# Three buffers for the slots' gathered rows and one for their outputs, in place of two and two

## What is computed

```python
def _L0_ffn_ref(x, gate_w, w1, b1, w2, b2, shared_w1, shared_b1, shared_w2, shared_b2):
    xf = x.reshape(-1, D)                      # 2048 rows of 512
    logits = xf @ gate_w
    top_logits, top_idx = jax.lax.top_k(logits, K)       # K = 2 of 8 experts
    top_gates = jax.nn.softmax(top_logits, axis=-1)
    ...
    h = gelu(jnp.einsum('nd,edh->neh', xf, w1) + b1)     # hidden size 256
    out_e = jnp.einsum('neh,ehd->ned', h, w2) + b2
    routed = jnp.einsum('ne,ned->nd', gates, out_e)
    shared = gelu(xf @ shared_w1 + shared_b1) @ shared_w2 + shared_b2
    return (routed + shared).reshape(B, S, D)
```

## Time and profile before

| what | us |
|---|---|
| median of three runs | 1681.28 |
| lowest and highest of them | 1679.48, 1681.79 |
| the profiled execution, device time | 1685.41 |
| its span, first to last instruction | 1683.7 |
| stage of the slots, from the first gather to the last y_out | 215.9 to 398.4 |

### The profile page before, as it was taken

The page is one execution under the profiler, slowest core; times in us unless marked ns, Lnnn a source line. Parts: engine busy times, 40 slices in busy tenths (PEclk is TensorE's granted clock), DMA queues, the critical chain, the costliest instruction groups (busy, mean ns, idle before and its releaser), DMA issues.

```text
span 1683.7 us, 27163 instructions
## 1 busy us (share of the span) xinstructions
PE 1626.0 (97%) x9136; PEld 1334.5 (79%) x9136; DVE 1084.2 (64%) x2115; ACT 1105.8 (66%) x2983; POOL 488.2 (29%) x515
## 2 busy tenths in 40 slices
PE   7989979999999999999999999999999999999998
PEld 6878756666778888888888888788888788887887
DVE  6258845443996668777787776666666666788322
ACT  4364245553468988888888888787787787885100
POOL 1001123222524243343342432433433334331000
PEclk9999979999999999999999999999999999999999
DMA  7031638885773242373333353121152131110011
GB/s 270 26 107 51 256 133 299 302 302 177 262 238 119 82 161 84 132 294 125 132 139 130 132 224 121 56 89 56 49 201 102 39 113 56 38 45 1 25 38 38
DMA packets 75156, 220.72 MB, mean 131 GB/s; under 512 B 6368, under 2 KB 14560, under 8 KB 68640
## 3 DMA queue, kind: packets, MB, share of 16 engines
q1 hardware_dynamic: 69360, 200.61, 32.7%
q0 software_dynamic: 5680, 18.62, 3.6%
HBM read 158.65 MB, written 60.56 MB: 130 GB/s over the span
## 4 chain that ended last, share of the span: by engine, by line
PE 72%; DMA 6%; DVE 5%; ACT 4%; issue 1%; POOL 1%; ACTq 0%; DVEq 0%; POOLq 0%; SPq 0%
PE bank L2485 10%; PE bank L2486 10%; PE bank L2548 7%; PE bank L97 6%; PE bank L99 6%; PE bank L98 6%; PE bank L2566 6%; PE bank L2579 6%; DMA s_rows<-x_rows,t_tok 5%; PE bank L2537 5%; PE bank L2558 3%; PE bank L1396 2%; PE bank L1416 2%; DVE x_res L1754 1%; PE bank L1376 1%
## 5 line engine op out<-in xcount | busy, mean ns | idle before, releaser
L2817 DVE TENSOR_TENSOR t_hn<-bank,t_rs 128x256 f32<-128x256 f32 (+1 forms) x256 | 130.8, 553 | 138.7 <-POOL t_rs L2450 73.2
L2485 PE MATMUL bank<-t_slot,t_x_q 128*128 128x512 f32 x512 | 205.8, 402 | 0.0
L2447 POOL TENSOR_SCALAR t_ve<-t_ss 128x4 f32<-128x4 f32 (+1 forms) x128 | 26.1, 204 | 615.5 <-DVE t_ss L2813 608.0
L2486 PE MATMUL bank<-t_slot,t_x_q 128*128 128x512 f32 x512 | 200.3, 391 | 0.0
L2706 ACT ACTIVATE t_sc<-bank,t_mx 128x128 f32<-128x128 f32 x512 | 184.4, 456 | 3.2 <-DVE t_mx L2837 3.2
L2450 POOL TENSOR_TENSOR t_rs<-t_ve,t_mhalf 128x4 f32<-128x4 f32 (+1 forms) x128 | 171.2, 1337 | 10.7
L2706 ACT ACTIVATION_READ_ACCUMULATOR t_sc<-bank,t_mx 128x1 f32 x512 | 151.8, 296 | 0.0
L2744 ACT ACTIVATE t_y<-bank,smooth 128x128 bf16<-128x128 f32 x512 | 139.7, 402 | 1.9 <-PE bank L2566 1.9
L2548 PEld LDWEIGHTS bank<-t_hT 128*128 128x128 f32 x1024 | 120.0, 191 | 17.0 <-ACT t_hT L2733 16.5
L2548 PE MATMUL bank<-t_hT 128*128 128x128 f32 x1024 | 131.0, 281 | 2.3 <-ACT t_hT L2733 2.3
L2486 PE MATMUL bank<-t_slot,t_x_kv 128*128 128x256 f32 x512 | 125.6, 283 | 0.0
(11 more groups left out here) (344 smaller groups left out, 4165.5 us busy)
## 6 DMA issues: line engine op xcount, KB each, us to landing
t_slot<-w_ready SPq DMA_DIRECT2D x16, 2048.0 KB, 9.3
t_xh<-xq_scratch SPq DMA_DIRECT2D x64, 512.0 KB, 3.6
t_cr<-in_ctxT_dram SPq DMA_DIRECT2D x64, 256.0 KB, 2.7
y_rows<-s_y SPq DMA_DIRECT2D x39, 256.0 KB
e_w<-in_w_units_dram SPq DMA_DIRECT2D x8, 1024.0 KB, 12.2
w_rows<-in_w_qkv_dram SPq DMA_DIRECT2D x8, 1024.0 KB, 6.2
w_ready<-w_hi SPq DMA_DIRECT2D x8, 1024.0 KB, 5.0
w_ready<-w_lo SPq DMA_DIRECT2D x8, 1024.0 KB
```

What stands on the lines that cost most here:

```text
L2485: nc.tensor.matmul(out, x_in[:, k, :], w[0][:, k, a:b], start=k == 0, stop=False)
L2486: last = nc.tensor.matmul(out, x_in[:, k, :], w[1][:, k, a:b], start=False, stop=k == KT - 1)
L2817: nc.vector.tensor_tensor(hn[:, lo:hi, :], b3[bk][:, 0:hi - lo, :], rs[:, lo:hi].unsqueeze(2).broadcast_to([P, hi - lo, P]), ALU.mult).the ...
```

## The change

The bytes are the same: three `rows` buffers (152, 154, 168) and one `y` buffer (170) take the place of two and two. The gather of slot s waits for turn(s-3) instead of turn(s-2). `y_out(s)` waits for the landing of the store of slot s-1 instead of s-2. One more semaphore counts the third gather buffer. No instruction changes its place on any engine; only buffers, semaphores and what is waited for differ.

```diff
-        self.rows = [mem.at(f"s_rows{i}", 152 + 2 * i, [P, D]) for i in range(2)]
+        self.rows = [mem.at(f"s_rows{i}", kb, [P, D]) for i, kb in enumerate((152, 154, 168))]
...
-        self.y = [mem.at(f"s_y{i}", 168 + 2 * i, [P, D]) for i in range(2)]
-        (rows_in0, rows_in1, self.turned, self.xT_in, self.up_ps, self.h_in, self.hturned, self.g_in, self.y_ps, self.y_in,
+        self.y = mem.at("s_y", 170, [P, D])
+        (rows_in0, rows_in1, rows_in2, self.turned, self.xT_in, self.up_ps, self.h_in, self.hturned, self.g_in, self.y_ps, self.y_in,
...
         for s in range(SLOTS_N):
-            if s >= 2:
-                pool.wait_ge(self.turned, s - 1)
+            if s >= 3:
+                pool.wait_ge(self.turned, s - 2)
             self.nc.gpsimd.indirect_dma_start(
-                self.rows[s % 2][:], None, self.env.dram["x_rows"],
-                bass.IndirectOffsetOnAxis(ap=self.route.tok[:, s:s + 1], axis=0)).then_inc(self.rows_in[s % 2], 16)
+                self.rows[s % 3][:], None, self.env.dram["x_rows"],
+                bass.IndirectOffsetOnAxis(ap=self.route.tok[:, s:s + 1], axis=0)).then_inc(self.rows_in[s % 3], 16)
 
     def turn(self, pe, s):
-        pe.wait_ge(self.rows_in[s % 2], 16 * (s // 2) + 16)
+        pe.wait_ge(self.rows_in[s % 3], 16 * (s // 3) + 16)
...
         def y_out(s):
             act.wait_ge(self.y_ps, s + 1)
-            if s >= 2:
-                act.wait_ge(self.y_st[s % 2], 16 * (s // 2))
-            nc.scalar.activation(self.y[s % 2][:], env.bank[6 + s % 2][:], ACT.Copy).then_inc(self.y_in, 1)
+            if s >= 1:
+                act.wait_ge(self.y_st[(s - 1) % 2], 16 * ((s - 1) // 2 + 1))
+            nc.scalar.activation(self.y[:], env.bank[6 + s % 2][:], ACT.Copy).then_inc(self.y_in, 1)
...
-            sp.dma_start(self.env.dram["y_rows"][s * P:(s + 1) * P, :], self.y[s % 2][:]).then_inc(self.y_st[s % 2], 16)
+            sp.dma_start(self.env.dram["y_rows"][s * P:(s + 1) * P, :], self.y[:]).then_inc(self.y_st[s % 2], 16)
```

More of the change, by code:

```diff
@@ L1351, in __init__ @@
         self.hT = [mem.at(f"s_hT{i}", 162 + i, [P, HT, P]) for i in range(2)]
-        self.y = [mem.at(f"s_y{i}", 168 + 2 * i, [P, D]) for i in range(2)]
-        (rows_in0, rows_in1, self.turned, self.xT_in, self.up_ps, self.h_in, self.hturned, self.g_in, self.y_ps, self.y_in,
+        self.y = mem.at("s_y", 170, [P, D])
+        (rows_in0, rows_in1, rows_in2, self.turned, self.xT_in, self.up_ps, self.h_in, self.hturned, self.g_in, self.y_ps, self.y_in,
          y_st0, y_st1) = (ctx.enter_context(nc.semaphore("s_" + n)) for n in (
-             "rows_in0", "rows_in1", "turned", "xT_in", "up_ps", "h_in", "hturned", "g_in", "y_ps", "y_in",
+             "rows_in0", "rows_in1", "rows_in2", "turned", "xT_in", "up_ps", "h_in", "hturned", "g_in", "y_ps", "y_in",
              "y_st0", "y_st1"))
-        self.rows_in, self.y_st = (rows_in0, rows_in1), (y_st0, y_st1)
+        self.rows_in, self.y_st = (rows_in0, rows_in1, rows_in2), (y_st0, y_st1)
         self.bases = {}
@@ L1375, in turn @@
         for k in range(KT):
-            last = self.nc.tensor.transpose(self.env.bank[s % 2][:, ramp(k)], self.rows[s % 2][:, ramp(k)],
+            last = self.nc.tensor.transpose(self.env.bank[s % 2][:, ramp(k)], self.rows[s % 3][:, ramp(k)],
                                             self.env.ident[:])
```

## The result

| kernel | median us | lowest to highest | runs |
|---|---|---|---|
| before | 1681.28 | 1679.48 to 1684.28 | 7 |
| changed | 1688.46 | 1684.23 to 1692.15 | 7 |

The changed kernel is slower by a ratio of 1.0034, 95% interval 1.0018 to 1.0050: 5.7 us, between 3 and 8. The forecast was 1690 us, with a range of 1679 to 1698.

The account below looks back on a forecast made before the run. PE work bounds the kernel, so the slots' end shifts its end about one for one. Gains of 12.4 us against a 19.3 us ring net 9 us slower: 1685.4 to 1694.4, less 4.1 for the median, 1690 us; range 1679 to 1698.

Parts of the forecast that it names:

- The early gain: At slot 4, gather issued before two 1 MB loads: PE turns 2.8 us earlier, clock staying at 2.4 GHz saves 1.75.
- The late gathers: From turn(5) to turn(38), gathers of `s_rows` cost 7.8 us; the third buffer removes all of it.
- The ring: In the slots' stage, y_out, store, landing, y_out closes through the big transfers: 19.3 us per four slots against PE's 16.4.
- Stretch A: y_out(4k) to y_out(4k+2), whose y store queues behind the `w_hi` and `w_lo` stores: 10.7 us against 8.2 unhindered.
- Stretch B: y_out(4k+2) to y_out(4k+4), whose y store queues behind the 1 MB load: 8.6 us.
- The sum: y_out(4) at 249.4, y_out(36) at 402.0 where it was 392.73; the rest follows as before, 9 us net cost.
- The reason in the queue: On SP's queue, descriptors go in ring order, so a y store waits for all SP issued before it, up to 2 MB.
- The forecast's case: In the slots' stage, four slots take between 18.4 and 20.5 us; chance 62%.
- rival 2: Slots' stage: four slots take 17.5 to 18.4 us, gains and cost cancel, within 3.4 us of before, 1681; chance 22%.
- Rival 1: y stores served beside the big ones land within 3.5 us, y_out never waits: -12.4 us, 1669; chance 8%.
- Rival 3: PE idles in each group and its clock falls, 1.75 us each; at 20.5 us per four slots, 1699 or more; 8%.
- the signs to look for: ACT's new wait at L1462, largest at slots 4k+2 (about 2.5 us) and 4k+4; PE's waits moved to `s_xT`; period 19.3.

Follow-up runs that it names:

- the second pair: Kernel before and changed kernel, both word for word, measured and traced again; changed kernel 1689.38 us, ratio 1.0034 to before.
- the output side alone: One output buffer with two gather buffers kept, against the kernel before; 1694.20 us, ratio 1.0068.
- the first experiment: Three gather buffers, two output buffers, only experts 0 to 3 picked (output not the reference's), against the kernel before; 1674.85 us, ratio 0.9943.

## Why the prediction held, and where it did not

**The early gain.** Forecast 2.8 + 1.75 = 4.55 us, and right. Both parts lie between turn(3) and turn(5): the kernel before takes 12.80 us there (228.67 to 241.47), the changed one 8.21 (226.89 to 235.10), 4.6 less. In the second pair it is 14.55 and 8.21. y_out(4) moved by more in the first pair, 6.4 us, because turn(0) was 0.7 us earlier already and turn(0) to turn(3) 1.1 shorter; in the second pair both differ the other way, and it moved 4.2. The kernel with the output side alone, which lacks the early gather, has y_out(4) at 254.13.

**The late gathers.** The forecast was 7.8 us, all gone. PE's waits for `s_rows` are down to the first slots in every kernel with three gather buffers. Both gains together were to be 12.4 us; the experiment with them alone gives 9.6 (6.7 to 12.6), a little less, in part because the late gathers differ between executions: the second trace of before has groups 0.4 us shorter than the first, 3.2 us over eight of them.

**The ring.** The loop was right, its terms were mis-sized, and their sum was 1 us or more too long. Stretch A was put at 10.7 us; the first two steps of the table give 9.9 and 10.0. Stretch B was put at 8.6; the last two give 8.0 and 8.3. The ring is 17.9 and 18.35 us where I had 19.3. Term by term, as the mean of eight in the first trace of the changed kernel: from the issue of `w_hi` to the landing of `w_lo` 7.9 us (7.3 to 9.9), where I had 9.1; a load 5.6, where I had 6.9; what the `y` store adds behind them 0.9 and 1.3, where I had 0.5 and 0.6.

In part the 9.1 was misread. I took the issue of the load for the landing of `w_lo`, but SP issues the load only after the store of slot 4k+2. In the kernel before it still had to wait for `w_lo` in five of the eight places (SP's own waits, us, times, longest):

```profile
SPq L136 <- DMA w_ready<-w_lo: 3.9, 4, 1.8
...
SPq L1314 <- DMA w_ready<-w_lo: 0.2, 1, 0.2
```

In the other three, the shortest of 8.3 us among them, `w_lo` had landed earlier, and the reading is the pace of y_out. Why the loads are shorter is not shown; the third gather buffer is not needed for it, since the output side alone, with two, has a median of 5.4 us. The bounds, 17.4 to 21.5, held the ring.

**The sum.** By the profiled execution alone the sum fails: y_out(36), forecast at 402.0, was at 390.86, as the row shows, and 1.9 us earlier than before's.

```profile
390.86 0.60 ACT L1462 ACTIVATE s_y<-bank 128x512 f32<-128x512 f32 x1 [2.89 <-DMA y_rows<-s_y]
```

In the second trace it is at 395.6, and before's second at 388.5: 7.1 us later. Over both pairs that is 2.6 us later, against 5.7 (3 to 8) by the runs and 9 by the forecast. The mis-sized term is the ring: the sum had the eight groups at 152.6 us (402.0 less 249.4), and they measured 143.3 and 146.8. With these 7.5 us less, and a start 1.2 us earlier, y_out(36) comes at 393.3, the mean of the two traces. The sum would then have said nearly 0 against before's profiled execution of 1685.4 us.

That the forecast of 1690 still came within 2 us is in part luck, a second error of the other sign. Before's profiled execution was 4.1 us above its median, and I took these 4.1 us off the changed kernel too, as if both had them. In good part they were late gathers (the groups of its second trace are 3.2 us shorter in all), and the changed kernel has none to lose. So: 9 us too much up to y_out(36), 4 too little for the base. The last 3 us, from 1685.4 to 1688.5, I can't assign; the changed kernel's two traces are of 1684.23 and 1689.28 us, in the mean 2 under its medians, so two may be too few to tell.

**The reason in the queue.** I wrote that a `y` store waits for what SP queued before it, by place in the queue. The kernel with the y stores on ACT's own queue shows that this step named the wrong thing, at slot 5: 6.8 us there, 7.1 here. In the forecast the sum was the same by either, because SP's transfers come first in both. The Trainium skill (DMA: Bandwidth & Descriptors, queues, rings and completion order) says that a DMA engine takes the queues of different issuers in turn, packet by packet. For a store issued behind 2 MB of another queue these runs don't agree with what I took from it, a landing within some 3.5 us: its first packets moved after 258.5, 3.6 us or more from its issue. For a store issued at the same moment as a load (262.33) they agree, with 82 packets against 81, and it lands between the two extremes. Why the engines do the one and the other was not settled here.

**The rivals.** The forecast's case was a ring between 18.4 and 20.5 us, and I had called it wrong if the period stays under 18.4. It stayed under, at 17.91 and 18.35: the time lay in the range, but the ring was the one of rival 2 (17.5 to 18.4). Rival 2's time, within 3.4 us of before, fits the two pairs of traces (2.6 us) and not the runs (5.7). Rival 1 (the stores don't wait) is out by ACT's 57 us. Rival 3's fall of the clock happened in full only with the y stores on ACT's queue. Of the signs to look for, I had not named the wait at slot 4k+3: the copy there starts only 2.95 us after the last, so even a lone store of 2.2 us shows.

## What to carry to other kernels

Before taking a buffer away, ask what must finish before its next write. If that is a DMA, cost its landing with everything that the DMA engines are given before it, from any queue (here a queue of its own did not help), and add up the loop of waits that closes through it: when that loop is longer than the busiest engine's period, it sets the pace, and shifting one transfer in it only moves the wait. The buffer to take is one whose reader is done soon after, as PE was with `s_xT`. And where a stage hangs on the luck of transfers, compare many runs: here one trace of each kernel had the sign wrong.

## What the runs showed of the hardware

- A 256 KB store that SP issued behind 2 MB of its own landed 7.0 us after issue, and 2.2 us when nothing was ahead. From another queue, behind the same 2 MB, the next copy could start 6.8 us after the issue; for the first 3.6 us none of its packets moved (q1 at 101.1% of the engines in 257 to 258.5, q10 absent). Issued together with a 1 MB load, the two queues moved 82 and 81 packets in 2 us, and the next copy could start 4.9 us after the issue.
- The DMA engines carried 325 GB/s in a group of the first experiment without ACT or PE waiting for them, in a stage where late gathers at 295 GB/s had looked like a shortage of bandwidth.
- After 3.7 us of idle time on PE its matmuls ran at 1.2 GHz (granted clock 0.50, 3.78 us for eight in place of 1.99). Waits of 0.6 and 1.0 us, as in the changed kernel at 260.91 and 266.30, left them at 1.99.
